# Attention loop of a conv + block attention + LoRA layer: the output sums placed between the first unit and the second query/key product of each double step

## The reference, cut to what matters

```python
# x: (2, 1024, 1024); everything is float32
def attn(inputs, ...):
    x = conv1d(inputs, conv_w, width 3, 'SAME') + conv_b       # 1024 -> 768
    q, k, v = split(x, 3)                                      # 256 each, in blocks of 128 rows
    qh, kh, vh = q @ wq + bq, k @ wk + bk, v @ wv + bv         # 16 heads of 64
    scores = where(causal, (qh / 8) @ kh.T, -1e9)              # per head, 128 x 128
    o = softmax(scores) @ vh
    o = sum over heads of o_h @ wo_h + bo                      # 256: the "output sums"
    return o @ proj_w + proj_b
x = x + attn(layernorm(x), ...)
x = x + ffn(layernorm(x), ...)   # one dense product and four gated rank-8 experts
```

## Time and profile before

| | |
|---|---|
| median of three runs | 812.07 us |
| profiled execution: time, span | 811.95 us, 810.2 us |
| TensorE matmuls busy | 779.5 us, 96% of the span |
| TensorE weight loads | 704.1 us, 87% |
| VectorE, ScalarE, GpSimd busy | 61%, 47%, 24% |
| chain that ended last | PE 68%, DVE 21%, ACT 6%, issue 3%, POOL 2% |

### The profile page before, as it was taken

One profiled execution on the slowest core, in us unless ns is written; L12 is line 12 of the kernel. 1 busy time (PEld: TensorE's weight loads), 2 busy tenths in 40 slices (PEclk: granted clock), 3 DMA queues, 4 the chain that ended last, 5 costly groups with the idle time before them and its releaser, 6 DMA issues.

```text
span 810.2 us, 14378 instructions
## 1 busy us (share of the span) xinstructions
PE 779.5 (96%) x5266; PEld 704.1 (87%) x5266; DVE 491.9 (61%) x1392; ACT 384.4 (47%) x1052; POOL 196.4 (24%) x184
## 2 busy tenths in 40 slices
PE   4999999999999889999999999999899999999996
PEld 3898888777878778999999999898789999999996
DVE  6999994889877566454545454646775444444441
ACT  5953343244335777676767676767741111111010
POOL 2300102222330234343434343443201010000000
PEclk9999999999999999999999999999999999999999
DMA  8746735433346140403071424020423131323201
GB/s 333 264 131 195 253 101 190 171 116 119 118 149 235 40 157 1 145 1 144 2 299 54 99 106 144 1 106 2 163 72 104 53 104 54 105 59 98 78 27 52
DMA packets 41370, 94.04 MB, mean 116 GB/s; under 512 B 9299, under 2 KB 18387, under 8 KB 40020
## 3 DMA queue, kind: packets, MB, share of 16 engines
q1 hardware_dynamic: 38996, 84.73, 31.2%
q0 software_dynamic: 2304, 8.39, 2.5%
HBM read 66.63 MB, written 26.08 MB: 114 GB/s over the span
## 4 chain that ended last, share of the span: by engine, by line
PE 68%; DVE 21%; ACT 6%; issue 3%; POOL 2%; DMA 0%; DVEq 0%; ACTq 0%; POOLq 0%
PE net_psum L63 16%; PE net_psum L65 16%; PE net_psum L64 16%; PE net_psum L1299 4%; PE net_psum L1310 3%; PE net_psum L1322 3%; DVE x_lo L899 2%; ACT pr L640 2%; PE net_psum L1350 2%; PE net_psum L1351 2%; PE net_psum L1352 2%; PE net_psum L1385 2%; POOL raw L486 1%; DVE raw L906 1%; DVE ua L861 1%
## 5 line engine op out<-in xcount | busy, mean ns | idle before, releaser
L63 PE MATMUL net_psum<-fw_hi,xT_hi 128*128 128x354 f32 (+1 forms) x384 | 126.1, 328 | 0.4 <-DVE fw_lo L1105 0.4
L65 PE MATMUL net_psum<-fw_hi,xT_lo 128*128 128x354 f32 (+1 forms) x384 | 124.4, 324 | 0.0
L64 PE MATMUL net_psum<-fw_lo,xT_hi 128*128 128x354 f32 (+1 forms) x384 | 124.2, 324 | 0.0
L510 POOL TENSOR_TENSOR pr<-pr,rrec 128x512 f32<-128x512 f32 x64 | 66.5, 1040 | 210.0 <-DVE rrec L978 207.0
L640 ACT ACTIVATE pr<-pr,negmax 128x128 f32<-128x128 f32 x256 | 99.0, 395 | 1.4 <-DVE negmax L970 1.4
L1239 PE MATMUL net_psum<-ua,wa 128*128 128x256 f32 x384 | 83.8, 379 | 0.5 <-DVE ua L864 0.5
L1239 PEld LDWEIGHTS net_psum<-ua,wa 128*128 128x128 f32 x384 | 72.6, 190 | 10.4 <-issue 0.7
L970 DVE CUSTOM_DVE_ANT_0 pr<-net_psum,mask 128x128 f32<-128x128 f32 x256 | 57.1, 286 | 40.1 <-PE net_psum L1299 40.1
L63 PE MATMUL net_psum<-c_hi,wqk_hi 128*128 128x256 f32 x256 | 74.5, 291 | 4.8 <-ACT kf L649 3.3
L63 PE MATMUL net_psum<-x_hi,w_hi 128*128 128x512 f32 x192 | 76.8, 400 | 1.7 <-DVE w_lo L913 1.5
L486 POOL TENSOR_TENSOR raw<-raw 128x512 f32<-128x512 f32 x24 | 36.8, 1533 | 161.3 <-ACT raw L589 161.3
(11 more groups left out here) (177 smaller groups left out, 1790.6 us busy)
## 6 DMA issues: line engine op xcount, KB each, us to landing
wa<-in_conv_w SPq DMA_DIRECT2D x24, 512.0 KB, 4.0
raw<-in_conv_w SPq DMA_DIRECT2D x24, 384.0 KB, 3.8
xn<-in_x SPq DMA_DIRECT2D x16, 512.0 KB, 10.1
xr<-in_x SPq DMA_DIRECT2D x8, 1024.0 KB, 5.0
x_scratch<-xr SPq DMA_DIRECT2D x8, 1024.0 KB, 4.1
x1t<-x_scratch SPq DMA_DIRECT2D x16, 512.0 KB, 4.1
out<-y POOLq DMA_DIRECT2D x16, 512.0 KB, 5.0
c_raw<-c_scratch SPq DMA_DIRECT2D x7, 768.0 KB, 4.7
```

The lines of the kernel that those rows point to most:

```text
L63: pe.matmul(out, w_hi, x_hi, start=first, stop=False)
L64: pe.matmul(out, w_hi, x_lo, start=False, stop=False)
L65: return pe.matmul(out, w_lo, x_hi, start=False, stop=last)
L510: pool.tensor_tensor(pr[:, jj % 4], pr[:, jj % 4], rrec[:, jj % 4].unsqueeze(2).to_broadcast([P, UN, P]), ALU.mult).then_inc(s["p_ready"], 1)
```

## The change

In `attention_pair(D)` of TensorE's queue the output sums of the pair of step D-3 are issued before `queries_keys(2 * D + 1)` and unit 1 and no longer behind them. The other engines' queues stay as they are. No instruction is added or taken away.

```diff
                 if D != 2:
                     run_unit(D, 0)
+                for jj in pair_of(D - PV):
+                    output_sums(jj)
                 if D < ND:
                     queries_keys(2 * D + 1)
                 run_unit(D, 1)
-                for jj in pair_of(D - PV):
-                    output_sums(jj)
```

## The result

The changed kernel takes 815.59 us, the median of five runs (814.5 to 815.9), against 812.07 us before: a ratio of 1.0045, 95% interval 1.0034 to 1.0056. It is 3.5 us slower. The profiled execution took 815.65 us, 3.7 us above that of before (span 813.8 against 810.2 us).

The account below looks back on a forecast made before the run. TensorE waits for nothing in a regular step; its largest waits were 3.3 us for `kf` and 3.2 us for `oT_lo`. 1.3 + 1.2 + 0.65 + 0.5 + 0.1 = 3.75 us on 811.95 gave 815.7 us, range 813.0 to 818.2.

Parts of the forecast that it names:

- Regular steps: Steps without extra work: no new wait, `oT_lo` margin 0.6 us; zero, within 0.5 us either way for changes of kind.
- Step 4, the order: Step 4: output sums wait 3.55 us for `oT_lo`, the second product follows them; 1.3 us later, bounds 1.1 and 1.5.
- Step 4, the clock: Step 4: the 3.55 us idle time brings the clock down to 1.2 GHz; 1.2 us, bounds 0 and 1.7.
- Steps 6 to 7: VectorE's `pw_lo` stands behind GpSimd's `c_lo`, so `projection` waits for late `a_low`; 0.65 us, bounds 0 and 3.0.
- Rival D: Step 6: GpSimd gets the port again before the waiting `pw_lo`; 818.1 us, chance 0.08.
- Steps 26 to 27: Tile 1's statistics stand behind unit 1's later evacuation, so `projection` starts late; 0.5 us, bounds 0 and 0.8.
- End of the loop: ACT's `kf` of the last job comes 1.4 us later, with work behind it; 0.1 us, bounds -0.2 and 0.5.
- A: Step 4: the clock stays up; 814.5 us, chance 0.17.
- B: Only step 4's 1.3 us come, without the clock and with VectorE's waits covered; 813.3 us, chance 0.10.
- F: Whole kernel: the new order has no effect, the engines absorb it; 812.1 us, chance 0.05.
- C: Steps 3 and 4: the sums fill the waits for `kf`, and both vanish; 810.1 us, faster, chance 0.05.
- E: Every step: `kf` of the second product is late; 818.5 us, chance 0.05.

Follow-up runs that it names:

- the fill: Changed kernel plus transposes nobody reads, in step 4 ahead of the output sums: 44 took 814.47 us, 31 took 814.92 us (ratio 1.0042).
- step 4 alone: New order in step 4 only, the old order in all other steps: 815.39 us, ratio 1.0050 to the kernel before.

## Why the prediction was right

Forecast were 815.7 us and measured 815.6, and the mechanism holds too: the named waits came in the named steps, and the clock fell where it was said to fall. That the numbers agree to 0.1 us is in part luck, since the five times of the changed kernel run from 814.5 to 815.9 us and the median of before moved between 811.4 and 812.3 us. The parts:

- **Regular steps.** Zero, as forecast. The 0.6 us margin of `oT_lo` was found to the tenth, and the test with 27 steps in the new order gave a ratio of 1.0000. The two changes of kind (unit to scores, sums to scores) do cancel: in the trace of that kernel all steps together make -0.04 us. Step 3 came as forecast: 0.93 us of waiting for `kf` became 1.02 us for `oT_lo`, and the scores moved by under 0.1 us.
- **Step 4, the order.** Forecast 1.3 us, measured 1.36 with the fill. The wait came out at 3.55 us as worked out. Of the 0.93 us from the product's end to the second half of the scores only 0.28 are a wait, because the first half of the scores fills the rest; the sum went to the second half and so holds.
- **Step 4, the clock.** Forecast 1.2 us within 0 and 1.7; measured 2.78 - 1.36 = 1.4 in the profiled execution, 3.00 - 1.36 = 1.6 with step 4 alone, and 3.82 - 1.36 = 2.5 in one execution. The upper bound of 1.7 was wrong: it took for granted that the low level lasts once as long as in step 33. In executions that kept the clock up, the lower bound of 0 may hold.
- **Steps 6 to 7.** Forecast 0.65 us, measured 0.64. `a_lo` was to be done at 318.9; it was done at 321.45, of which 2.53 us are the delay that the step began with. The projection's start moved by 0.65 us. The wait that the trace shows, 0.49 us, is counted from the modelled end of the matmul before, so it is shorter than the 0.6 that was said to show. The queueing of `pw_lo` behind `c_lo` was read from two rows of other places, and the 1.99 us came where 1.9 was named. By the Trainium skill, "SBUF — State Buffer", section "SBUF: two separate sides", the first to start keeps the port for its instruction. The trace agrees: `pw_lo` ended 1.08 us behind `c_lo`, and it takes 1.20 us alone. The page leaves open who is next; here the waiting VectorE operation was next and GpSimd's stood (3.38 us), as in rows 7 and 9. Rival D falls.
- **Steps 26 to 27.** Forecast 0.5 us, measured 0.69. The masked scores moved by the 1.2 us that were worked out. That the wait came out at 0.44 us, where 0.45 was forecast, is luck: the forecast was the shift of the projection's start, and that is 0.60 us. The missing 0.16 lies on VectorE. `a_low` starts 1.02 us behind the first of the masked scores (523.41 to 524.43), where the forecast took the 0.85 of the earlier trace rows. It is 1.02 in all five profiled kernels that have the new order in step 26 and `tile_statistics` behind it, and 0.85 in the eight others. Why the masked scores take longer there is open.
- **End of the loop.** Forecast +0.1 us. Measured from the scores of step 31 to the end of the span it is -0.2 us: -0.11 in step 31, and -0.13 behind it. The second of these also holds the clock's fall in step 33, which both profiled executions have but not at the same place.
- **The rivals.** A (the clock stays up) holds in no profiled execution that has the new order in step 4 and no fill. In executions without a trace it may: with step 4 alone one took 813.71 us at a mean granted clock of 0.997, where four took 815.0 to 815.5 at 0.994 or 0.995, and the changed kernel's fastest, 814.5 us, had 0.997 against 0.993 to 0.996. B falls by the low clock and the two waits for `a_lo`, F by the ratio. C and E are excluded by the trace: the wait for `kf` went, but the wait for `oT_lo` took its place, and regular steps have no wait.
- **The ranges.** The forecast's own range of 814.3 to 817.2 us doesn't follow from its terms: with 1.2 less or 0.5 more of clock and 0.5 us either way for the changes of kind it is 814.0 to 816.7. The measured median lies in both.

One thing was missed: the prediction read the low clock behind step 33 in the one execution that was profiled, at 811.95 us, and took it for the kernel's. Others of the same kernel had it not. The sum was made against an execution of the slower group. It came out right because the changed kernel's profiled execution had it too.

## What to carry to other kernels

When a step is moved ahead in an in-order queue, look for its latest input in every step and not only in the typical one. Here 27 of 30 steps cost nothing (the one that was measured had 0.6 us to spare), and the whole loss lay in three steps at the seams, where another engine still had work left from the part before or had extra work behind the evacuation that was moved. A wait of 2 us or more on TensorE can cost more than its length, since the clock may fall behind it: 0.8 to 2.5 us here. In step 33 a fill with unread work took 1.3 us off the median; in step 4 only the trace shows what it gave. Where the times of one kernel stand in two groups, compare the granted clock behind its longest waits first.

## What the runs showed of the hardware

- Around the end of an idle time of 3.55 us TensorE went to 1.2 GHz for 3.4 us in the changed kernel and for 6.8 us in another with the same wait; it did so for 6.8 us too around the end of the 5.2 us wait for `kf`. With an idle time of 2.0 to 2.3 us it did so in some executions and not in others. The price was 1.4, 1.6 and 2.5 us for the longer wait, and 0.8 to 1.7 us for the shorter.
- A transpose of 128x128 float32 took 0.107 us when issued back to back in the fill, against 0.117 us for a matmul of 256 columns: half the columns took 91% of the time.
- With both engines' operations waiting for the same port, the first was the one that had been waiting: `pw_lo` 1.99 us and behind it GpSimd's bias sum 3.38 us, where they take 1.2 and 2.4 alone.
